# One decoder layer on one core: keys and queries quantised in their PSUM banks, low parts on GpSimd, and the last query tile turned inside the scores

## What is computed

```
q = LN(x) @ Wq + bq ;  k, v = split(ctx @ Wkv + bkv)      # 16 heads of 32; 1024 queries, 2048 keys
q = fq_sym(q * scale, axis=-1)       # s = max|q| / 127 per row and head; round(q / s) * s
k = fq_sym(k, axis=-1)
v = fq_sym(v, axis=keys)             # one step for each of the 512 columns, over all 2048 keys
p = fq_unsigned(softmax(q k^T), axis=-1)
x = x + (p @ v) @ Wp + bp
```

## Time and profile before

| | us |
|---|---|
| median of 3 runs (1194.95 to 1198.07) | 1196.88 |
| the profiled execution, its own time | 1200.02 |
| its span | 1198.3 |
| busy in the span: PE, DVE, ACT, POOL | 978.5, 834.3, 646.0, 271.8 |
| keys and values, first key matmul to the last query's copy | 203.9 to 358.6 |
| scores, 128 units | 359.0 to about 828 |

### The profile page before, as it was taken

How to read it: one execution, slowest core, us unless ns; L and a number is a source line. 1 busy time by engine, 2 the same in 40 slices (tenths; PEclk the granted TensorE clock), 3 DMA queues, 4 the chain that set the end, 5 groups by cost and what they waited for, 6 DMA issues and landing times. The chain is left out here.

```text
span 1198.3 us, 21781 instructions
## 1 busy us (share of the span) xinstructions
PE 978.5 (82%) x8049; PEld 667.7 (56%) x8049; DVE 834.3 (70%) x1398; ACT 646.0 (54%) x1040; POOL 271.8 (23%) x265
## 2 busy tenths in 40 slices
PE   4988987999877677767777767675889899999996
PEld 3744835888654444444444444444667666556665
DVE  6858656899888999999999999997634321111225
ACT  3453362455677888888888888885133012121220
POOL 1135054566407700000000000002524500000032
PEclk9999999999987999999999999998979899999998
DMA  8400002110000100000000000000040792221134
GB/s 315 167 1 1 1 1 105 55 36 19 8 1 1 46 1 1 0 0 0 0 0 0 0 0 0 0 0 1 24 157 2 292 404 89 83 102 62 62 93 145
DMA packets 24858, 68.19 MB, mean 57 GB/s; under 512 B 2722, under 2 KB 6818, under 8 KB 23778
## 3 DMA queue, kind: packets, MB, share of 16 engines
q1 hardware_dynamic: 20114, 52.48, 11.7%
q0 software_dynamic: 4400, 14.42, 3.7%
q10 hardware_dynamic: 288, 0.52, 0.2%
HBM read 49.07 MB, written 18.35 MB: 56 GB/s over the span
## 5 line engine op out<-in xcount | busy, mean ns | idle before, releaser
L1317 ACT ACTIVATE cs_p_int<-cs_s_b,cs_bias,cs_step_now 128x1024 int16<-128x1024 f32 x128 | 154.0, 1203 | 63.8 <-DVE cs_bias L1352 63.8
L1345 DVE TENSOR_REDUCE cs_top<-cs_s_b 128x1 f32<-128x512 f32 x256 | 164.7, 685 | 12.3 <-PE cs_s_b L1374 3.4
L1374 PE MATMUL cs_s_b<-k_parts,q_int 96*128 96x512 bf16 x256 | 80.0, 395 | 110.5 <-ACT cs_p_int L1317 110.4
L1382 PE MATMUL cs_tp<-ident,cs_p_int 128*128 128x128 f16 x2048 | 159.4, 222 | 2.9 <-ACT cs_pT L1323 1.1
L1333 DVE TENSOR_REDUCE cs_top<-cs_s_a 128x1 f32<-128x1024 f32 x128 | 155.5, 1215 | 4.3 <-PE cs_s_a L1374 4.3
L1317 ACT ACTIVATE cs_p_int<-cs_s_a,cs_bias,cs_step_now 128x1024 int16<-128x1024 f32 x128 | 152.8, 1194 | 0.0
L1382 PEld LDWEIGHTS cs_tp<-ident,cs_p_int 128*128 128x128 f16 x2048 | 121.6, 98 | 48.5 <-issue 44.7
L2198 PE MATMUL ff_h<-ff_experts,ff_zgT 128*128 x368 | 112.9, 460 | 0.9 <-ACT ff_zgT L1837 0.9
L1480 POOL TENSOR_TENSOR co_o<-co_o,v_step 128x512 f32<-128x512 f32 x8 | 10.6, 1330 | 414.3 <-DVE co_o L1502 414.3
L1374 PE MATMUL cs_s_a<-k_parts,q_int 96*128 96x512 bf16 x256 | 80.3, 396 | 22.7 <-ACT cs_p_int L1317 17.9
L1360 DVE COPY cs_pT<-cs_tp 128x1024 int16<-128x1024 int16 x128 | 87.1, 680 | 3.3 <-PE cs_tp L1382 3.1
(11 more groups left out here) (287 smaller groups left out, 2120.7 us busy)
## 6 DMA issues: line engine op xcount, KB each, us to landing
ff_experts<-in_experts_dram SPq DMA_DIRECT2D x8, 2176.0 KB, 14.1
slots<-sa_zero SPq DMA_DIRECT2D x1, 5888.0 KB, 24.9
ff_zg<-slots POOLq DMA_DIRECT2D x23, 256.0 KB, 2.9
run_y<-ff_yv SPq DMA_DIRECT2D x23, 256.0 KB, 2.0
ff_raw<-in_weights_dram SPq DMA_DIRECT2D x6, 768.0 KB, 5.2
ck_raw<-in_ctxT_dram SPq DMA_DIRECT2D x8, 512.0 KB, 3.2
stage<-in_cwkv_dram SPq DMA_DIRECT2D x2, 1024.0 KB, 5.1
out_dram<-x_res SPq DMA_DIRECT2D x8, 256.0 KB, 2.0
```

The lines of the kernel that those rows point to most:

```text
L1317: nc.scalar.activation(p_int[:, u, half * HALF:(half + 1) * HALF], s[:, :], ACT.Exp, bias=bias[:, u:u + 1], scale=step_now[:, h:h + 1], ac ...
L1345: nc.vector.tensor_reduce(top[:, u, 1 + c:2 + c], s_b[:, c * 512:(c + 1) * 512], AX_X, ALU.max).then_inc(max_ok, 1)
L1374: ins = nc.tensor.matmul(s[:, c * 512:(c + 1) * 512], q_int[0:3 * D, t, h, :], k_parts[0:3 * D, h, keys:keys + 512], start=True, stop=True)
L1382: ins = nc.tensor.transpose(tp[:, k, :], p_int[:, u, key:key + P].bitcast(F16), ident16[:, :])
```

## The change

In `quantise_keys` and `quantise_queries` the tile `kf` is gone: the bias is added and the scaling done in place in the PSUM bank `kb`, which DVE then rounds from; PE may refill the bank only after the rounding (`kint_ok`, `q1_ok`) instead of after the bias add (`kf_ok`, `qf_ok`). The low parts of the keys (`low_keys`) and of the query weights (`low_query_weights`, four pieces in place of two on DVE) move from DVE to POOL; `low_keys` of tile n - 3 stands between `low_context` of n and `key_rests` of n - 2. `q_step` and `q_nstep` are written by POOL (`keep_steps`), and DVE waits for them from query tile 2 on. `low_z` of tile c + 2 stands inside `quantise_queries` of c. The largest of a turn is taken in the first tile of the next one. The last query tile's rounded values go to `q_last`; in `cross_scores` ACT triples them, PE turns them behind the first unit's scores and ACT copies them to `q_int`, before its first exponential. The reciprocal `v_rstep` is made in four pieces at the end of score units 0 to 3, and POOL waits for its piece. The core of the diff:

```diff
@@ GpSimd @@
+            def low_keys(u, n):
+                pool.wait_ge(mid_ok, n + 1)
+                nc.gpsimd.tensor_tensor(parts[:, u, :, 2, :], rest[:, u, :, :], parts[:, u, :, 1, :],
+                                        ALU.subtract).then_inc(lo_ok, 1)
+
+            def low_query_weights(k):
+                pool.wait_ge(wq_hi_ok, 1)
+                nc.gpsimd.tensor_tensor(wq_lo[:, k, :], wq_raw[:, k, :], wq_hi[:, k, :].bitcast(F32),
+                                        ALU.subtract).then_inc(wq_lo_ok, 1)
+
+            def keep_steps(c):
+                pool.wait_ge(step_ok, c + 1)
+                nc.gpsimd.tensor_scalar(q_step[:, c, :], step[:, c % 2, :], scale, 0.0, ALU.mult, ALU.add).then_inc(steps_kept, 1)
+                nc.gpsimd.tensor_scalar(q_nstep[:, c, :], step[:, c % 2, :], -scale, 0.0, ALU.mult, ALU.add)\
+                    .then_inc(steps_kept, 1)
...
                     pool.wait_ge(lo_ok, n - 1)
+                    pool.wait_ge(tr_ok, n - 1)
...
                 low_context(t, n)
+                if there(n - 3, KT):
+                    low_keys(1 - t % 2, n - 3)
                 if there(n - 2, KT):
                     key_rests(t % 2, n - 2)
+                if isinstance(n, int) and n >= LAST:
+                    low_query_weights(n - LAST)
+            nc.gpsimd.memset(own_top[:, :], 0.0).then_inc(top_ok, 1)
...
             norm(0)
+            low_keys(1, KT - 3)
             key_rests(0, KT - 2)
             norm(1)
+            low_keys(0, KT - 2)
             key_rests(1, KT - 1)
-            for c in range(2, TT):
+            low_keys(1, KT - 1)
+            norm(2)
+            norm(3)
+            for c in range(4, TT):
+                keep_steps(c - 4)
                 norm(c)
-            pool.wait_ge(top_ok, TURNS)
+            keep_steps(TT - 4)
+            pool.wait_ge(top_ok, TURNS + 1)
             nc.gpsimd.partition_all_reduce(v_step[:, :], own_top[:, :], P, ABSMAX).then_inc(all_top, 1)
+            for c in range(TT - 3, TT):
+                keep_steps(c)
+            pool.wait_ge(steps_kept, 2 * TT)
...
@@ ScalarE @@
-            for c in range(2, TT):
+            for c in range(2, TT - 1):
                 if c + 2 < TT:
                     high_z(c + 2)
                 keep_queries(c - 2)
                 triple(c)
+            keep_queries(TT - 3)
             keep_queries(TT - 2)
-            keep_queries(TT - 1)
...
@@ VectorE, quantise_keys @@
-                nc.vector.tensor_tensor(kf[:, :, :], heads(kb[u][:, :]), heads(bias[:, 0:C]), ALU.add).then_inc(kf_ok, 1)
-                v_.wait_ge(kf_ok, n + 1)
-                link(nc.vector.tensor_reduce(rstep[:, :], kf[:, :, :], AX_X, ALU.max, apply_absolute_value=True))
+                kf = heads(kb[u][:, :])
+                link(nc.vector.tensor_tensor(kf, kf, heads(bias[:, 0:C]), ALU.add))
+                link(nc.vector.tensor_reduce(rstep[:, :], kf, AX_X, ALU.max, apply_absolute_value=True))
...
-                link(nc.vector.tensor_tensor(kf[:, :, :], kf[:, :, :], per_head(rstep[:, :]), ALU.mult))
-                nc.vector.tensor_scalar(kint[:, u, :, :], kf[:, :, :], MAGIC, MAGIC, ALU.add, ALU.subtract).then_inc(kint_ok, 1)
+                link(nc.vector.tensor_tensor(kf, kf, per_head(rstep[:, :]), ALU.mult))
+                nc.vector.tensor_scalar(kint[:, u, :, :], kf, MAGIC, MAGIC, ALU.add, ALU.subtract).then_inc(kint_ok, 1)
...
@@ VectorE, step_of @@
                 quantise_keys(u, n)
+                turn_done = t == 0 and not (isinstance(n, int) and n == 0)
+                if turn_done:
+                    v_.wait_ge(vf_ok, n)
+                    v_.wait_ge(top_ok, turn)
                 values(u, n)
-                turn_done = t == LOOP_TILES - 1 and not (isinstance(n, int) and n == KT - 1)
                 if turn_done:
-                    v_.wait_ge(vf_ok, n + 1)
-                    if not isinstance(n, int):
-                        v_.wait_ge(top_ok, turn)
-                if there(n - 1, KT):
-                    low_keys(1 - u, n - 1)
-                if turn_done:
-                    if isinstance(n, int):
-                        largest_of_turn(own_top, 0, slice(0, C), top_ok)
-                    else:
-                        largest_of_turn(turn_top, n - t, slice(0, C), turn_ok)
-                        keep_largest(turn, turn)
+                    largest_of_turn(n - LOOP_TILES, slice(0, C))
+                    keep_largest(turn, turn)
...
-                if isinstance(n, int) and LAST <= n < LAST + 2:
-                    ks = slice(2 * (n - LAST), 2 * (n - LAST) + 2)
-                    v_.wait_ge(wq_hi_ok, 1)
-                    nc.vector.tensor_tensor(wq_lo[:, ks, :], wq_raw[:, ks, :], wq_hi[:, ks, :].bitcast(F32),
-                                            ALU.subtract).then_inc(wq_lo_ok, 1)
...
@@ VectorE, quantise_queries @@
-                if c == 0:
-                    v_.wait_ge(kint_ok, KT)
-                nc.vector.tensor_tensor(kf[:, :, :], heads(kb[c % 2][:, :]), heads(bias_q), ALU.add).then_inc(qf_ok, 1)
-                v_.wait_ge(qf_ok, c + 1)
-                link(nc.vector.tensor_reduce(rstep[:, :], kf[:, :, :], AX_X, ALU.max, apply_absolute_value=True))
+                qf = heads(kb[c % 2][:, :])
+                link(nc.vector.tensor_tensor(qf, qf, heads(bias_q), ALU.add))
+                link(nc.vector.tensor_reduce(rstep[:, :], qf, AX_X, ALU.max, apply_absolute_value=True))
+                if c + 2 < TT:
+                    low_z(c + 2)
                 if c < 2:
                     v_.wait_ge(kq_ok, KT - 1 + c)
+                else:
+                    v_.wait_ge(steps_kept, 2 * (c - 1))
                 link(nc.vector.tensor_scalar(step[:, c % 2, :], rstep[:, :], 1.0 / QMAX, Q_FLOOR / scale, ALU.mult, ALU.max))
-                nc.vector.tensor_scalar(q_step[:, c, :], step[:, c % 2, :], scale, None, ALU.mult)
-                nc.vector.tensor_scalar(q_nstep[:, c, :], step[:, c % 2, :], -scale, None, ALU.mult)
-                link(nc.vector.reciprocal(rstep[:, :], step[:, c % 2, :]))
-                link(nc.vector.tensor_tensor(kf[:, :, :], kf[:, :, :], per_head(rstep[:, :]), ALU.mult))
-                if c >= 2:
-                    v_.wait_ge(q3_ok, c - 1)
-                nc.vector.tensor_scalar(q1[:, c % 2, :, :], kf[:, :, :], MAGIC, MAGIC, ALU.add, ALU.subtract).then_inc(q1_ok, 1)
+                step_made = nc.vector.reciprocal(rstep[:, :], step[:, c % 2, :])
+                step_made.then_inc(step_ok, 1)
+                v_.wait_ge(step_ok, c + 1)
+                link(nc.vector.tensor_tensor(qf, qf, per_head(rstep[:, :]), ALU.mult))
+                if c == TT - 1:
+                    v_.wait_ge(zT_ok, TT)
+                    v_.wait_ge(zlo_ok, TT)
+                    into = q_last
+                else:
+                    if c >= 2:
+                        v_.wait_ge(q3_ok, c - 1)
+                    into = q1[:, c % 2, :, :]
+                nc.vector.tensor_scalar(into, qf, MAGIC, MAGIC, ALU.add, ALU.subtract).then_inc(q1_ok, 1)
...
@@ VectorE, after the tiles @@
             quantise_queries(0)
-            low_keys(1, KT - 1)
-            low_z(2)
             for c in range(1, TT):
                 quantise_queries(c)
-                if c + 2 < TT:
-                    low_z(c + 2)
...
+                if c == TT - 2:
+                    v_.wait_ge(all_top, 1)
+                    nc.vector.tensor_scalar(v_step[:, :], v_step[:, :], 1.0 / QMAX, Q_FLOOR, ALU.mult, ALU.max)\
+                        .then_inc(all_top, 1)
             v_.wait_ge(all_top, 2)
-            v_.wait_ge(zT_ok, TT)
-            nc.vector.reciprocal(v_rstep, v_step[:, :]).then_inc(all_top, 1)
-            v_.wait_ge(all_top, 3)
...
@@ TensorE @@
-                    pe.wait_ge(kf_ok, n - 1)
+                    pe.wait_ge(kint_ok, n - 1)
...
-                    pe.wait_ge(kf_ok, KT - 1 + c)
+                    pe.wait_ge(kint_ok, KT - 1 + c)
                 else:
-                    pe.wait_ge(qf_ok, c - 1)
-                pe.wait_ge(wq_lo_ok, 2)
+                    pe.wait_ge(q1_ok, c - 1)
+                pe.wait_ge(wq_lo_ok, CK)
...
             turn_queries(TT - 2)
-            turn_queries(TT - 1)
...
@@ cross_scores: GpSimd, ScalarE, VectorE, TensorE @@
+                pool.wait_ge(rstep_ok, h // HG + 1)
...
+            nc.scalar.copy(q3, q_last.unsqueeze(2).broadcast_to([P, H, 3, D])).then_inc(q3_ok, 1)
             nc.scalar.activation(table[:, :], ident16[:, 0:1], ACT.Exp)
+            act.wait_ge(tq_ok, 1)
+            nc.scalar.copy(q_int[0:3 * D, TT - 1, :, :], tq[:, :, :]).then_inc(q_kept, 1)
...
+                if isinstance(n, int) and n < HG:
+                    cols = slice(n * P, (n + 1) * P)
+                    nc.vector.reciprocal(v_rstep[:, cols], v_step[:, cols]).then_inc(rstep_ok, 1)
...
             scores(0, 0, s_a[0], 0, sa_ok)
+            scores(0, 0, s_b, 1, sb_ok, each_bank=True)
```

(21 more changed lines are left out.)

39 lines of the change are left out of this document (17 added, 22 removed).

## The result

The kernel after takes 1203.8 us, the median of 5 runs (1201.95 to 1205.26), against 1196.88 for the kernel before (also 5 runs, 1194.95 to 1198.07): the ratio is 1.0061, with a 95% interval of 1.0045 to 1.0078. That is slower by 0.3 to 0.8%, inside the predicted range, on the predicted side, and 2.6 us longer than predicted.

The account below looks back on a forecast made before the run. PE bounds the key tiles, DVE the scores. The block (+4.3 - 0.5 - 3.8 + 1.0 = +1.0) and the scores (+1.2, +2.1) sum to +4.3 us: 1201.2 from 1196.88, range 1193.3 to 1205.5.

Parts of the forecast that it names:

- a rival that had 5%: Query tiles' end: POOL loads code between all-reduce and `keep_steps`, tile 7 waits 3.2 us longer; +7.5 us, 1204.4; 5%.
- Key tiles, +1.6: Key tiles: `low_keys` on POOL makes each of 9 or 10 tiles 0.17 us longer, +1.6 us.
- The circle of 6.60 us: Key tiles: POOL and ACT's loop per tile, 5.44 us plus 1.16 for `low_keys`, 0.17 over PE's 6.43.
- the short lengths hold throughout: Key tiles: POOL's kq always takes 1.04 us, not 1.50, as DVE hardly keeps operations with two large SBUF inputs.
- Into the queries, +4.3: From keys to query tile 1: late normalising of tiles 0 and 2 delays tile 1 by 4.3 us, the 1.6 included.
- The chain through ACT: Normalising query tile 2 queues on POOL behind key tile 15's `low_keys` and ACT's links; z(2) 4.5 us later.
- Clock, +1.0: After PE's new 4 us wait before z(2), half of a slow-clock stretch: +1.0 us (ends 0 and 1.6).
- Query tiles, -0.5: Query tiles 1 to 7: 0 per tile, an earlier `low_z` for tile 7 gains 0.5 us.
- Tail, -3.8: Block's end: from tile 7's start ACT only copies tiles 5 and 6, 4.5 us instead of 8.3: -3.8 us.
- Scores, +3.3: Score units: first exponential later, +1.2 us, and four reciprocals on DVE, the first free, half the second, +2.1 us.
- the prediction's own list of signs: Findings in the changed profile that would prove it wrong, among them POOL still for 6 us or more behind the all-reduce.
- the first rival's -4.7: Into the queries: POOL's queue is not late, tile 1 starts at 320.8 as before; -4.7 us, 1192.2; 15%.

Follow-up runs that it names:

- e2: The kernel after, with query tile 2 normalised right behind tile 1 on POOL, ahead of the low parts of key tiles 14 and 15; 1199.17 us, ratio 1.0034.
- e4: The kernel before, with only the last query tile and the four reciprocals moved into the scores; ratio 0.9997 to before.
- e12: The kernel before with the last query tile and four reciprocals in the scores, measured again on another chip; ratio 0.9984.
- e6: The kernel after, with the steps of query tiles 5, 6 and 7 copied by DVE instead of POOL; ratio 1.0054 to before.
- e11: The kernel after, unchanged, for a second profiled execution; ratio 1.0056 to before.
- e8: The kernel before, unchanged, for a second profiled execution without a ratio; key block 155.3 us.
- e5: The kernel before, with only the adding, scaling and rounding of keys and queries done in PSUM, without the SBUF copy; ratio 1.0008.

## Why the prediction was right, and where it was not

Sign and place were right, and so was the mechanism in the main; in the tail a rival that had 5% came true, and in the key tiles a collision stayed that had been taken as gone. The sizes of five terms were not right. Predicted 4.3 us; measured 8.1 in the two stages and 6.9 in the medians.

*Key tiles, +1.6.* The circle of 6.60 us was measured at 6.57, but in one tile of four kq takes 1.50 instead of 1.05 (at 245.31, 272.18 and 298.90) and the tile 7.03, and in another the tile takes 6.71. Each time DVE runs `keep_largest` beside it (L1018, at 245.01, 271.86 and 298.59), a maximum of two SBUF tiles. Four tiles take 26.9 us instead of 25.9, so the ten tiles cost 2.5. The step that failed is "the short lengths hold throughout". That the meeting with L1018 lengthens kq is read from its coming together each time; no run took L1018 away. The Trainium skill's rule ("GPSIMD Engine Reference", Key points) on instructions with two SBUF inputs agrees with both: the short lengths stand beside the in-place operations, the long ones beside the one left that has two SBUF inputs.

*Into the queries, +4.3.* z(0) came 4.4 and 5.1 us late (forecast 3.3), z(2) 6.3 and 6.6 (forecast 4.5), tile 1 8.1 (126.9 and 126.6 against 118.7). The chain through ACT was as forecast, link by link, and e2 shows that it alone was worth 3.2; it began later, by the key tiles and z(0), and the clock fell right in tile 1's product, 1.6 us of the 8.1 (6.05 us from z(2) to tile 1, against 4.4 before).

*Clock, +1.0.* It is that 1.6, behind the new wait for z(2), as written; it was the upper end of what I had allowed. It is contained in the 8.1 and not added again.

*Query tiles, -0.5.* They are 4.99 us apart instead of 4.86: the rounding's 0.26 outweighs the two small operations. From tile 1 to 7 are 28.5 to 29.3 us, against 27.9 to 29.5.

*Tail, -3.8.* Measured 6.7 and 7.7 us from tile 7's start to the first score, instead of 8.6: -1 to -2. The -3.8 itself was well sized: e4 and e12, which have no operation behind the all-reduce, show -3.3 and -3.8. The 5% rival, POOL's stand behind the all-reduce, took 2.35 and 3.40 of it; e6 gives 1.7 and 2.7 of it back (5.0 us). The diff had put the copies of tiles 5 to 7 behind the all-reduce, the same hole had been read in the earlier trace rows, and I doubted it only for the form of the instruction. Its chance should have been most of the forecast's. The Trainium skill ("GPSIMD Engine Reference", Instruction dispatch) has about 6 us for the first call to a freshly loaded kernel. The trace agrees in kind, for a plain one-tensor operation too, and measures some 1 us more: 6.8 to 7.6 in five executions.

*Scores, +3.3.* Both terms came about as worked out, and then a part of them was given back for a reason that no row of the prediction held. The first exponential came 5.46 us into the scores. Of the four reciprocals (0.94 us each) the first fell into a wait; each of the next three lengthens its unit to 4.17 us, from one maximum of `s_a` to the next, where before has 3.4 to 3.9. The maximum of unit 7 comes 29.6 and 29.3 us behind the first score (after, e11), instead of 26.4 and 26.0 (before, e8): 3.0 to 3.6 late. So DVE bounds these units too for the most part, as the earlier trace rows had it for the later ones.

Units 16 to 19 give 1.4 to 2.1 of it back: 12.6 and 13.3 us in before and e8, 11.26 in after and e11. Timeline of POOL and DVE there, first of before:

```profile
415.69 4.51 POOL L1293 TENSOR_TENSOR wp_lo<-stage,wp_hi 128x2048 fp32r<-128x2048 f32 x1
...
419.12 1.12 DVE L1341 COPY cs_nstep_now<-q_nstep 128x16 f32 x1
```

and of after:

```profile
424.37 4.51 POOL L1319 TENSOR_TENSOR wp_lo<-stage,wp_hi 128x2048 fp32r<-128x2048 f32 x1
...
431.67 0.17 DVE L1370 COPY cs_nstep_now<-q_nstep 128x16 f32 x1
```

In before the copy begins while POOL makes the next weights' low part, and ends 0.04 us behind it; PE then waits, and the granted clock falls to 0.72 (422 to 428). In the three executions with the old beginning of the scores (before, e8, e5) this copy takes 1.12, 1.81 and 1.45 us; in the eleven others 0.17, and their units 16 to 19 take 11.3. There the copy comes after POOL's operation has ended. That is a meeting of two engines that the later start of the scores' units happens to miss, and no saving that the change aimed at; no run moved POOL's operation by itself, so the cause is read from where the two meet in the 14 traces. What is left at the end is 1.3 us.

So the block was put 5.8 us too low (6.8 against 1.0) and the scores 2.0 too high. The rest, from 8.1 to the 6.9 of the medians, lies in stretches that the change does not touch.

That the total came within 2.6 us is in part luck: the two errors have opposite signs, the scores' one comes from the missed meeting at unit 16, and by the prediction's own list of signs (POOL standing still for 6 us or more behind the all-reduce) its account of the tail was wrong. The low end of its range was also worked out wrongly, without effect here: half of the first rival's -4.7 is not -3.6.

## What to carry to other kernels

Before an operation is moved to an idle engine, write down that engine's circle with the others in us and its queue in order: an engine 23% busy bounded a stage here, and some 5 of 7 us came from the order of its queue, from what stood behind the moved operations. Look also for small operations of the neighbour that fall beside a long one of POOL: one of 0.17 us became 1.1 to 1.8 long here. Nothing that another engine waits for belongs behind a partition all-reduce. And judge a part of 1 us by its stage between two marks in several profiles; the spans differed by as much without it.
